# Six parts of the output projection moved into a batch's last attention pair, and GpSimd's ones and residual moved behind the centering

## The reference, cut to what matters

```python
b, s, _ = x.shape                       # of _layernorm(x)
kqv = x @ Wqkv + bqkv
kqv = kqv.reshape(b, s, 3, 16, 32)
q, k, v = kqv[:, :, 0], kqv[:, :, 1], kqv[:, :, 2]
scores = jnp.einsum('bsnh,btnh->bnst', k, q) / math.sqrt(32)
scores = jnp.triu(scores) + -10000.0 * jnp.tril(ones, k=-1)
attn = jax.nn.softmax(scores, axis=2)
out = jnp.einsum('bnkq,bknh->bqnh', attn, v)
x = x + out.reshape(b, s, 512) @ Wo + bo
```

## Time and profile before

| | |
|---|---|
| median of 3 executions | 3064.85 us (3061.29 to 3065.31) |
| profiled execution, its own time | 3057.86 us |
| its span, first to last instruction | 3056.1 us |
| mean granted TensorE clock | 0.984 of full |
| TensorE matmul busy | 2831.2 us (93%) |
| VectorE busy | 1953.7 us (64%) |
| ScalarE busy | 1202.4 us (39%) |
| GpSimd busy | 869.8 us (28%) |

### The profile page before, as it was taken

The page is one execution under the profiler, slowest core; times in us unless marked ns, Lnnn a source line. Parts: engine busy times, 40 slices in busy tenths (PEclk is TensorE's granted clock), DMA queues, the critical chain, the costliest instruction groups (busy, mean ns, idle before and its releaser), DMA issues.

```text
span 3056.1 us, 59013 instructions
## 1 busy us (share of the span) xinstructions
PE 2831.2 (93%) x20444; PEld 2054.0 (67%) x20444; DVE 1953.7 (64%) x2926; ACT 1202.4 (39%) x1913; POOL 869.8 (28%) x1305
## 2 busy tenths in 40 slices
PE   3898899999898899999988989999998998999998
PEld 3655578777665558777765546877776555787776
DVE  2556465777755655777665557477777555757777
ACT  2245334444225434444323552444432444344442
POOL 2313212433212212333321231233333132123332
PEclk7999999999999999999989999999999999999999
DMA  9322111111233202111123220211123230111112
GB/s 346 96 64 66 39 44 42 46 52 51 81 71 72 53 22 56 49 47 47 41 91 79 55 50 21 63 50 49 40 71 91 50 80 18 54 50 47 46 46 80
DMA packets 163796, 192.16 MB, mean 63 GB/s; under 512 B 43962, under 2 KB 103994, under 8 KB 161786
## 3 DMA queue, kind: packets, MB, share of 16 engines
q1 hardware_dynamic: 155486, 175.31, 21.0%
q10 hardware_dynamic: 8096, 14.16, 1.5%
HBM read 106.99 MB, written 23.36 MB: 43 GB/s over the span
## 4 chain that ended last, share of the span: by engine, by line
PE 73%; DVE 14%; issue 5%; DMA 2%; ACT 2%; SPq 1%; POOL 1%; ACTq 1%; DVEq 0%; POOLq 0%
PE ps L765 16%; PE ps L766 15%; PE ps L767 15%; DVE mneg L1720 6%; PE ps L886 4%; PE ps L1153 4%; PE ps L943 3%; PE ps L925 2%; PE ps L1139 2%; PE ps L1162 2%; PE ps L1203 2%; PE ps L881 2%; DVE X L1574 1%; ACT PR L1352 1%; PE ps L1173 1%
## 5 line engine op out<-in xcount | busy, mean ns | idle before, releaser
L765 PE MATMUL ps<-uh,win 128*128 128x512 f32 x1536 | 623.3, 406 | 0.6
L766 PE MATMUL ps<-ul,win 128*128 128x512 f32 x1536 | 602.0, 392 | 0.0
L767 PE MATMUL ps<-uh,win 128*128 128x512 f32 x1536 | 600.9, 391 | 0.0
L1720 DVE TENSOR_REDUCE mneg<-ps 128x1 f32<-128x128 f32 (+7 forms) x512 | 367.5, 753 | 348.9 <-PE ps L886 347.5
L1352 ACT ACTIVATE PR<-ps 128x1024 f32<-128x1024 f32 (+3 forms) x384 | 293.0, 807 | 307.1 <-PE ps L925 280.2
L2091 POOL TENSOR_SCALAR_AFFINE_SELECT LM<-LM 128x512 f32<-128x512 f32 x256 | 211.5, 837 | 501.5 <-ACT LM L1469 501.5
L765 PEld LDWEIGHTS ps<-uh,win 128*128 128x128 f32 x1536 | 289.0, 188 | 72.5 <-issue 9.5
L1834 DVE TENSOR_TENSOR LM<-ps,LM 128x512 f32<-128x512 f32 x256 | 170.4, 686 | 258.4 <-PE ps L1153 213.9
L767 PEld LDWEIGHTS ps<-uh,win 128*128 128x128 f32 x1536 | 288.9, 188 | 64.4
L766 PEld LDWEIGHTS ps<-ul,win 128*128 128x128 f32 x1536 | 289.6, 189 | 53.5
L943 PE MATMUL ps<-PR,V 128*32 128x512 f32 (+3 forms) x1536 | 282.6, 493 | 6.6 <-ACT OT L1362 4.1
(11 more groups left out here) (228 smaller groups left out, 5146.2 us busy)
## 6 DMA issues: line engine op xcount, KB each, us to landing
raw<-in_t SPq DMA_DIRECT2D x128, 256.0 KB, 2.8
QS<-EV SPq DMA_DIRECT2D x192, 128.0 KB, 2.5
KS<-EV SPq DMA_DIRECT2D x168, 128.0 KB, 2.6
in_t<-tiles ACTq DMA_DIRECT2D x10, 1024.0 KB, 9.5
XN<-in_L_attn_a_x_dram SPq DMA_DIRECT2D x40, 256.0 KB, 5.9
win_raw<-in_L_attn_a_Wqkv_dram SPq DMA_DIRECT2D x34, 256.0 KB, 3.5
win_raw<-in_t SPq DMA_DIRECT2D x32, 256.0 KB, 2.8
edec<-ed_t SPq DMA_DIRECT2D x512, 16.0 KB, 1.6
```

Source lines behind the costliest of these rows:

```text
L765: pe.matmul(dst, hi_l, hi_r, start=first, stop=False)
L766: pe.matmul(dst, hi_l, lo_r, start=False, stop=False)
L767: return pe.matmul(dst, lo_l, hi_r, start=False, stop=last)
L1720: dve.tensor_reduce(mneg[:, hh, t:t + 1], flat[:, off:off + (t + 1) * P], AX.X, ALU.max, negate=True).then_inc(a_max.sem, 1)
```

## The change

In the last pair of each batch, six parts of Wo's product, k = 0 to 2 of tiles 0 and 1 (`OUTPUT_PARTS`), are made inside the pair: one between the scores of units 2 and 3, and one after the scores of each of the five sessions, before that session's weighing. `row_product` leaves these six out. They write banks 0 and 1. The first waits for Wo's low part, for group 2's `ot_lo[0]`, and for ScalarE's copy of the last maxima out of bank 0. On GpSimd, one wait before the ones and the residual is for all eight low parts of the normalised input (`ln_lo`), where it was for its own second inverse roots (`ln_rstd`).

```diff
--- before.py
+++ after.py
@@ -32,6 +32,9 @@
 
 ORDER = [(0, 0), (0, 3), (0, 2), (0, 1), (1, 0), (1, 7), (1, 6), (1, 5), (1, 4), (1, 1), (1, 2), (1, 3)]
 UNITS = len(ORDER)
+
+
+OUTPUT_PARTS = [(t, k) for t in range(2) for k in range(3)]
 
 
 DIAGONAL = [u for u, (c, k) in enumerate(ORDER) if k >= 4 * c]
@@ -810,7 +813,7 @@
                         pe.matmul(ps[:, 4 + q % 4, :], hgT[:, q % 2, :], wu[:, :], start=True, stop=False)
                         pe.matmul(ps[:, 4 + q % 4, :], w3T[:, q % 2, :], bu3[:, :], start=False, stop=True).then_inc(u_pe.sem, 1)
 
-            def row_product(product, n, ready_before, ready, ready_later=lambda: None):
+            def row_product(product, begun, n, ready_before, ready, ready_later=lambda: None):
 
                 def part(t, k):
                     return product(ps[:, t % 4, :], k, t * P, k == 0, k == KT - 1)
@@ -818,7 +821,8 @@
                 ready_before()
                 for t in range(4):
                     for k in range(KT - 1):
-                        part(t, k)
+                        if (t, k) not in begun:
+                            part(t, k)
                 ready()
                 for t in range(4):
                     part(t, KT - 1).then_inc(w_pe.sem, 1)
@@ -987,6 +991,17 @@
                 v_done.wait(pe, b, TT)
                 pe.sem_inc(s_tick, 1)
 
+                def output_product(dst, k, t0, first, end):
+                    return three(dst, oth[:, t0 // P, k * P:(k + 1) * P], OTL[:, k, t0:t0 + P], wo_high[:, k, :], wo_low[:, k, :], first, end)
+
+                def output_part(t, k):
+
+                    if (t, k) == (0, 0):
+                        wo_lo.wait(pe, b, 1)
+                        ot_lo[0].wait(pe, b * 4 + 2, 1)
+                        m_act.wait(pe, b * 8 + 7, 1)
+                    output_product(ps[:, t, :], k, t * P, k == 0, False)
+
                 for g in range(GROUPS):
                     for hf in range(2):
                         p = b * 8 + g * 2 + hf
@@ -997,9 +1012,13 @@
                                 group_scores_a(p + 1, pair + 1, FILLING[k][0])
                             if k == 0:
                                 scores_b(p, pair, (2,))
+                                if not ahead:
+                                    output_part(*OUTPUT_PARTS[0])
                                 scores_b(p, pair, (3,))
                             else:
                                 scores_b(p, pair, (2 * k + 2, 2 * k + 3))
+                            if not ahead:
+                                output_part(*OUTPUT_PARTS[k + 1])
                             if hf == 0 and g < GROUPS - 1 and k < 4:
                                 project(g + 1, k)
                             if ahead:
@@ -1013,9 +1032,7 @@
                             scores_b(p + 1, pair + 1, (0, 1))
 
                 wo_lo.wait(pe, b, 1)
-                row_product(lambda dst, k, t0, first, end:
-                            three(dst, oth[:, t0 // P, k * P:(k + 1) * P], OTL[:, k, t0:t0 + P], wo_high[:, k, :], wo_low[:, k, :], first, end),
-                            b * 2, lambda: ot_lo[0].wait(pe, b * 4 + 2, 1), lambda: ot_lo[0].wait(pe, b * 4 + 3, 1),
+                row_product(output_product, OUTPUT_PARTS, b * 2, lambda: ot_lo[0].wait(pe, b * 4 + 2, 1), lambda: ot_lo[0].wait(pe, b * 4 + 3, 1),
                             lambda: ot_lo[1].wait(pe, b * 4 + 3, 1))
 
                 pe.wait_ge(s_pre_st, 16 * 3)
@@ -1981,7 +1998,7 @@
             group_lo(0)
             with pool.Fori(0, NB) as b:
                 inverse_roots(b * 4, (1,))
-                until(ln_rstd, b * 4, 2)
+                until(ln_lo, b * 4, TT)
                 until(qkw_lo, b * 4, 1)
                 pool.wait_ge(s_pre_st, 16 * 3)
                 pool.sem_inc(s_tick, 1)
```

## The result

Timed side by side in five executions each, the changed kernel takes 3050.32 us (3046.29 to 3051.44), the kernel before 3065.31 us (3061.29 to 3071.8). The ratio is 0.995, interval 0.9939 to 0.9962: faster by 15 us, 0.5%. The forecast was 3056.4 us with a range from 3051.0, so the direction was right, the size was short by 6 us, and the time lies 0.7 us under the range. The changed kernel's profiled execution took 3050.32 us as well, 7.5 us less than the one of before (3057.86). The forecast's 8.5 us was near the difference of the two profiled executions and far from the difference of the medians; the experiments have to explain that.

What follows compares the result with a forecast made beforehand. TensorE, 73% of the chain's span, bounds the kernel through its idle time and the chains it waits for. Gains of 2.0 + 3.7 + 2.8 = 8.5 us off 3064.85 give 3056.4 us, range 3051.0 to 3063.5.

Steps and rivals of the forecast that it cites:

- I keep that offset: Whole kernel: the profiled execution lies 7.0 us under the median; that difference was carried unchanged into the forecast time.
- part one: Six product parts moved into each last pair: 4.24 us removed, 2.43 back, 1.3 new wait; 2.0 us gained in four batches.
- Sessions 0 to 4: Last pair's scores and weighings, followed session by session with the parts added: 2.43 of 4.24 us per batch come back.
- The new wait: TensorE before tile 4 in Wo's product, for group 3's second half: 1.3 us per batch, independent of the lateness.
- Part two: GpSimd's ones and residual moved behind the centerings at batch starts: costs nothing, gains 6.5 us, 3.7 gaps and 2.8 half clock.
- The excess of 6.50 us over batch 0: Starts of batches 1 to 3, tile 2's turn to group 0's last projection: 1.00 + 4.29 + 1.21 us, all taken as gain.
- The Trainium skill's rule on two SBUF inputs: VectorE instructions with two SBUF inputs contend with GpSimd SBUF reads; an overlap might cost up to 1.3 us each.
- the row on EV: Batch 0's residual ran over two projection low parts; the slowest of 64 took 753 ns against median 743, so no contention.
- Rival A: Batch 2's start: the clock's fall isn't recovered or turns up elsewhere; gain 5.7 us, 3059.2 us, chance 0.30.
- Rival B: Batch starts: unprofiled executions lose the clock in more, all recovered; one more fall of 2.8 us, 3053.5 us, chance 0.12.
- C: Last pair: no part is hidden; part one loses 5.2 us; 3066.3 us, or 3063.5 with the clock recovered, chance 0.12.
- D: Tile 4: clock falls behind the new wait, 2.8 us each, 11.2 in four batches; 3070.3 us, chance 0.06.

Runs made afterwards that it cites:

- the last experiment: Changed kernel with Wo's product's wait for group 3's second half moved from before tile 4 to before its last part: 3043.27 us, 0.9935; again 3045.74 us, 0.9936.
- second profile: The kernel before, run once more with no edit: 3064.22 us, ratio 1.0001 to before; its profiled execution took 3064.46 us.
- padding: Changed kernel plus four unused matmuls behind Wo's product, giving the saved time back: 3058.02 us, ratio 0.9965 to the kernel before.

## Why the prediction was wrong, point by point

Both mechanisms came as forecast: the parts fill gaps and expose a wait at tile 4, and the centerings run undisturbed. What failed is the sum. The step "I keep that offset" left the time between the profiled execution and the median outside the gain, part one was summed at 2.0 us where its stages give 3.6, and the falls that the parts spare stood in no term.

- **Sessions 0 to 4.** 2.43 us were to come back, 1.93 did. Against the forecast's times, with 0.60 added, the scores of units 4 and 5 came at 340.68 (340.87), of 6 and 7 at 343.47 (343.69), of 8 and 9 at 346.16 (346.56), of 10 and 11 at 349.19 (349.68), and the product at 354.58 (355.08). The 0.70 us of sessions 1 and 4 were right (0.67 and 0.69). Sessions 0 and 2 were each charged 0.2 us too much and session 3 0.1. The weighings of 0 and 2, taken as 1.29 and 1.32 us, took 1.21 and 1.22, and the scores and parts ahead of each took 0.1 us less than the listed lengths added up.
- **The new wait.** 1.3 us at tile 4, without a dependence on the lateness: right place and releaser, measured 1.15 as listed idle time. Hiding it as in the last experiment took 1.4 us out of the product, so 1.3 was near its cost. Net gain of part one by its stages: 0.9 us per batch, 3.6 in all, where I summed 2.0; the 0.5 us of the sessions make the difference.
- **Part one's other gain.** That the parts spare falls in the last pair and at the decay logits was in no term; the prediction put both at nothing. By the counts, 5 falls in six executions in the last pair cost 7.2 us together, 1.2 per execution, and 3.5 less 1.6 falls of 0.95 us at the decay logits are 1.8 per execution. With 3.6 this makes 6.6 us, against 7 to 9 measured by the medians.
- **Part two.** The mechanism, its cover and that it costs nothing were right. The excess of 6.50 us over batch 0 fell to 0.34 + 0.20 + 0.40 = 0.94 us. The Trainium skill's rule on two SBUF inputs (SBUF — State Buffer, Who interferes with whom) changed nothing in the new place, as the row on EV had said: after the change the 64 low parts take 742 ns at the median and 752 at most. But 6.50 was one execution's sum; the kernel before has 3 x 2.78 = 8.3 us in its second profile, so part two was undersized by 1 to 2 us. Rival A, the fall not recovered, is out at this place: between tile 2's turn and the projections, in batches 1 to 3, a fall began in 8 of 12 starts with the old wait and both works in front, and in none of 24 with the new one.
- **The offset.** This is the step that failed most: "I keep that offset", 7.0 us from the profiled execution to the median, as if all of it lay where the change doesn't reach. The second profile of the kernel before, near the median, shows 6.6 us. Of these 1.9 are at the starts, 1.0 in a last pair and 0.8 around the decay logits, 3.7 us at places where the change spares falls, so they belonged to the gain. The 2.6 us at the first turns and the 2.0 behind the state-space layer's product are not removed by it: the first turns take 27.2 and 29.8 us in the two profiles of before and 31.0 and 30.1 in those after. Here the first profile was a quick one by luck. The changed kernel has no such offset (3050.32 and 3050.32). Rival B named falls at the starts and allowed one more of 2.8 us; that was the right kind and too small, since the places of part one count as well.
- **Rivals C and D.** No. Some of each part was hidden but for sessions 1 and 4, and no fall followed the new wait of 1.15 us in any profiled execution. But the argument against D, that the last pair's gaps draw no fall, was true of the first profile alone: without the parts 5 of 24 have one.

Put together from two profiled executions of each kernel, stage by stage over four batches: from tile 2's turn to the first maxima 118.6 us became 110.8, pair and product 175.7 became 171.7, the first part of the decay logits' stage 135.6 became 134.2, and the first turns went from 28.5 to 30.6, 1.2 of it because batch 3's had kept its clock once. That is 11.1 us, and small differences elsewhere make it the 11.8 us between the profiled executions. The other 3 of the 15 come mostly from the first profile of before being a quick one. The second, at 3064.46 us near the median of 3065, lies 15.0 us over the two of the changed kernel: 8.7 us from tile 2's turn to the first maxima (1.0 of it a longer wait for a DMA in batch 2, which kernels with the new wait have at times too), 4.5 in pair and product, 1.8 around the decay logits, 1.2 behind the state-space layer's product, and 1.2 less in the rest. Against the 8.5 us of the forecast, part one's stages are 1.6 us more and the rest is mostly falls of the clock. This is one execution of the kernel before; most single executions were not profiled.

## What to carry to other kernels

Before a change is costed against one profiled execution that lies well off the median, ask what the others do differently; here over half of the difference lay where the change spares stalls. Work moved into another engine's gaps pays only where the gap stands at that spot: three of six parts brought twice the net gain of all six, and a wait that the shorter remainder exposed could be covered by waiting later. GpSimd work without a deadline belongs where it lengthens nothing of VectorE's that TensorE waits for, even if it is short.

## What the runs showed of the hardware

- A memset over one partition holds up a centering of 128 partitions until it ends: 1.69 us in place of 0.54, ended 0.29 us behind the memset. Eight adds stretch four centerings of a start to 0.70 to 1.44 us. The memset took 2.66 us with and 2.67 without a centering beside it, so there VectorE alone waited. The eight adds take 10.5 to 10.7 us beside centerings and 10.0 without, so there both did.
- Half-clock stretches come at a few places of the program in some executions and not in others, behind the same idle gap. At the decay logits it is the time elapsed since earlier changes of the clock that decides, in all 56 starts of the fourteen profiles: 0.8 us of padding, 36 us ahead, turned falls in 11 of 28 batches into falls in 4 of 4. The saving of 0.9 us per batch was thereby worth about twice itself here, and another saving could be worth less than itself.
